# Involution stage of a two-layer vision kernel: the next block's logit chain starts four taps before the slot, evenly spread, and the sums are turned back between two chains

## The reference, cut to what matters

```python
n, _, h, w = x.shape
x1 = conv1x1(x, w1, b1)
x2 = conv1x1(x, w2, b2)
x3 = conv1x1(x, w3, b3)
p = conv1x1(position(h, w, x.dtype), wp, bp)
sub2 = x1[:, :, None] - unfold_patches(x2)
subp = p[:, :, None] - unfold_patches(p)
...
y = jax.nn.relu(bn_eval(feat, bn1_g, bn1_b, bn1_m, bn1_v))
y = conv1x1(y, cw1)
y = jax.nn.relu(bn_eval(y, bn2_g, bn2_b, bn2_m, bn2_v))
wgt = conv1x1(y, cw2, cb2)
wgt = jax.nn.softmax(wgt, axis=2)
...
        out = out + patch * wgt[:, :, idx][:, :, None]
```

## Time and profile before

| | |
|---|---|
| median of 3 runs | 4714.37 us (4712.43 to 4714.96) |
| the profiled execution | 4718.02 us, span 4716.2 us |
| involution stage within it | about 180 to 2107 us |
| busy over the whole span | PE 88%, DVE 74%, ACT 45%, POOL 23% |
| mean granted TensorE clock | 0.961 |

### The profile page before, as it was taken

The page is one execution under the profiler, slowest core; times in us unless marked ns, Lnnn a source line. Parts: engine busy times, 40 slices in busy tenths (PEclk is TensorE's granted clock), DMA queues, the critical chain, the costliest instruction groups (busy, mean ns, idle before and its releaser), DMA issues. The chain is left out here.

```text
span 4716.2 us, 68009 instructions
## 1 busy us (share of the span) xinstructions
PE 4158.9 (88%) x25234; PEld 2496.8 (53%) x25234; DVE 3511.6 (74%) x3316; ACT 2110.5 (45%) x3376; POOL 1085.4 (23%) x426
## 2 busy tenths in 40 slices
PE   5789989899998989976889898898889879999999
PEld 2267777777777777763343433334344234444544
DVE  6179989899898989987566756756676358787877
ACT  1455545455554545423645455363544523232321
POOL 1265555555655555530000000000000000000000
PEclk9889999999999999998999999999999989999999
DMA  5400101101101011012011001102111010000100
GB/s 202 129 29 33 37 30 37 37 16 37 37 34 36 29 37 37 11 45 62 1 49 56 22 21 59 45 1 57 47 22 22 28 47 32 24 31 29 34 20 24
DMA packets 88774, 186.97 MB, mean 40 GB/s; under 512 B 14622, under 2 KB 78158, under 8 KB 85378
## 3 DMA queue, kind: packets, MB, share of 16 engines
q1 hardware_dynamic: 86274, 177.51, 11.9%
q0 software_dynamic: 1744, 4.89, 0.3%
q10 hardware_dynamic: 432, 0.20, 0.0%
HBM read 103.60 MB, written 59.70 MB: 35 GB/s over the span
## 5 line engine op out<-in xcount | busy, mean ns | idle before, releaser
L684 DVE TENSOR_TENSOR prod<-ps,win 128x1792 f32<-128x1792 f32 x686 | 1340.2, 2012 | 128.8 <-ACT ps L579 96.5
L752 PE MATMUL ps<-ident,prod 128*128 128x128 f32 x9604 | 1185.5, 279 | 150.4 <-DVE prod L684 126.5
L752 PEld LDWEIGHTS ps<-ident,prod 128*128 128x128 f32 x9604 | 1104.5, 144 | 313.5 <-DVE prod L684 173.0
L1129 ACT ACTIVATE phq<-ps 128x896 f32<-128x896 f32 x448 | 384.2, 917 | 200.3 <-PE ps L1390 199.5
L594 ACT ACTIVATE y<-ps,u2c,s2c 128x392 f32<-128x392 f32 x392 | 265.4, 677 | 442.3 <-PE ps L735 440.9
L1225 DVE TENSOR_TENSOR phk<-kv 128x2048 f32<-128x2048 f32 (+1 forms) x200 | 455.9, 2283 | 0.6
L470 POOL TENSOR_TENSOR lg<-lg,mx 128x1568 f32<-128x1568 f32 x98 | 348.7, 3569 | 338.1 <-DVE mx L673 338.1
L465 POOL TENSOR_TENSOR y<-a1w,x2w 128x1568 f32<-128x1568 f32 x98 | 320.3, 3269 | 427.8 <-PE ps L735 408.9
L1551 POOL MEMSET ones<- 128x128 bf16 x1 | 0.2, 204 | 1654.0 <-POOLq L894 1654.0
L734 PE MATMUL ps<-y,cw1bd 128*128 128x392 f32 x784 | 331.4, 505 | 52.3 <-ACT y L587 29.5
L1762 PE MATMUL ps<-xn,w_s 128*128 128x448 f32 x896 | 353.5, 549 | 6.2 <-ACT hid L1599 6.2
(11 more groups left out here) (220 smaller groups left out, 5058.9 us busy)
## 6 DMA issues: line engine op xcount, KB each, us to landing
win<-planes SPq DMA_DIRECT2D x14, 2480.0 KB, 9.4
qst<-qsp SPq DMA_DIRECT2D x96, 196.0 KB, 4.6
planes<-stage SPq DMA_DIRECT2D x7, 1984.0 KB, 7.0
xs<-in_x SPq DMA_DIRECT2D x8, 1568.0 KB, 21.1
conv_dram<-osb SPq DMA_DIRECT2D x14, 896.0 KB, 4.9
t<-in_x SPq DMA_DIRECT2D x28, 448.0 KB, 4.1
xn<-conv_dram SPq DMA_DIRECT2D x28, 448.0 KB, 6.9
t_dram<-tout SPq DMA_DIRECT2D x28, 448.0 KB, 2.9
```

The source lines that it names most:

```text
L684: v.tensor_tensor(prod[b.buf(t)][:].rearrange("p (s h w) -> p s h w", h=RW, w=W), w, xw, ALU.mult).then_inc(prod_ready, 1)
L752: mm = pe.matmul(acc[:, at:at + P], x[:, at:at + P], ident[:], start=(t == 0 and k % 4 == 0), stop=(t == NU - 1), is_transpose=True, skip_ ...
L1129: act.activation(dst, src, ACT.Square).then_inc(phq_done, 1)
```

## The change

`slot` gets a third block, `n`, whose chain begins in the last four taps: `CH_AT` goes from -4 to 39 in steps of 8/5 tap, so that chunks 0, 1 and 2 of the next block stand at taps 45, 46 and 48, and the last logits at tap 41. The running maxima and the fold (tap 43) move with it. The sums are turned back at taps 41 to 44, between the two chains, copied at 42 to 45, and scaled at 47; the inverse stands at tap 1 of the next slot. The denominators are added up in `osb` instead of `acct`. On GpSimd shifts 1 and 2 stand directly at the slot's start, behind shift 0, the first two subtractions of `n` stand behind `total`, and the exponential of row 1 moves from the last tap to the first tap of the next slot. The loads of x2, a1 and two feature rows move to the end of the slot before. The slot list has three slots ahead of the loop, five turns of two slots, and three behind it. The copies at the slot's end (`weights`) stay where they were.

```diff
@@ -327,20 +327,19 @@
 SUMC = SHARE * PW
 NBACK = (SUMC + 511) // 512
 HALF = 1024
-GAP = 8
-CH_AT = [1 + c * 6 // 5 for c in range(GAP)] + [16 + c * 6 // 5 for c in range(NCH - GAP)]
+FIRST = -4
+CH_AT = [FIRST + c * 8 // 5 for c in range(NCH)]
 LAST_LOGIT = CH_AT[-1] + 2
-LOGIT_AT = CH_AT[1:] + [LAST_LOGIT]
-MAX_AT = [min(LOGIT_AT[CPI * i + CPI - 1] + 3, LAST_LOGIT + 1) for i in range(K7)]
+MAX_AT = [CH_AT[CPI * i + CPI] + 3 if i + 1 < K7 else LAST_LOGIT + 1 for i in range(K7)]
 FOLD_AT = MAX_AT[-1] + 1
-EXP_NOW = {FOLD_AT + 3: 0, NU - 1: 1}
-EXP_NEXT = {3: 2, 5: 3, 9: 4, 16: 5, 22: 6}
-SHIFT_BEFORE = {1: (1,), 2: (2, 3), 3: (4,), 4: (5,), 5: (6,)}
-BACK_AT = [CH_AT[GAP] - 5 + p for p in range(NBACK)]
-RECIP_AT, SCALE_AT = BACK_AT[-1] + 3, BACK_AT[-1] + 5
+EXP_NOW = FOLD_AT + 3
+EXP_NEXT = {0: 1, 5: 2, 10: 3, 17: 4, 23: 5, 30: 6}
+BACK_AT = [LAST_LOGIT + p for p in range(NBACK)]
+RECIP_AT, SCALE_AT = 1, BACK_AT[-1] + 3
+FIRST_RELU = NU + FIRST - 3
 PAIRS = (TAPS + 1) // 2
-ADD_BEFORE = {4: (1, 2), 5: (3,), 6: (4, 5)}
 NADD = K7 + 3
+assert BACK_AT[-1] < NU + FIRST
...
         half = run[:, 0:3]
-        wsum = acct[:, 0:K7 * PW].rearrange("p (j x) -> p j x", x=PW)
+        wsum = osb[:, 0:K7 * PW].rearrange("p (j x) -> p j x", x=PW)
...
-            slot(Blk(0, 0), None)
-            slot(Blk(0, 1), Blk(0, 0))
-            with eng.Fori(0, NW // 2 - 1) as it:
-                slot(Blk(it, 2), Blk(it, 1))
-                slot(Blk(it, 3), Blk(it, 2))
-            slot(None, Blk(0, NW - 1))
+            slot(None, None, Blk(0, 0))
+            slot(Blk(0, 0), None, Blk(0, 1))
+            slot(Blk(0, 1), Blk(0, 0), Blk(0, 2))
+            with eng.Fori(0, NW // 2 - 2) as it:
+                slot(Blk(it, 2), Blk(it, 1), Blk(it, 3))
+                slot(Blk(it, 3), Blk(it, 2), Blk(it, 4))
+            slot(Blk(0, NW - 2), Blk(0, NW - 3), Blk(0, NW - 1))
+            slot(Blk(0, NW - 1), Blk(0, NW - 2), None)
+            slot(None, Blk(0, NW - 1), None)
...
-                        pool.wait_ge(turned, NBACK * b.n)
+                        pool.wait_ge(stored, 16 * b.n)
...
-            def slot(a, b):
-                for i in range(K7):
-                    if b:
-                        for k in SHIFT_BEFORE.get(i, ()):
-                            shift(b, k)
-                        for k in ADD_BEFORE.get(i, ()):
-                            add(b, k)
-                    if a:
-                        z(a, i)
+            def slot(a, b, n):
                 if b:
-                    add(b, K7 - 1)
+                    shift(b, 1)
+                    shift(b, 2)
+                if a:
+                    z(a, 2)
+                if b:
+                    shift(b, 3)
+                if a:
+                    z(a, 3)
+                if b:
+                    shift(b, 4)
+                    add(b, 1)
+                if a:
+                    z(a, 4)
+                if b:
+                    shift(b, 5)
+                    add(b, 2)
+                    add(b, 3)
+                if a:
+                    z(a, 5)
+                if b:
+                    shift(b, 6)
+                    add(b, 4)
+                if a:
+                    z(a, 6)
+                if b:
+                    add(b, 5)
+                    add(b, 6)
                     total(b)
+                if n:
+                    z(n, 0)
+                    z(n, 1)
                 if a:
                     shift(a, 0)
...
+            def slot(a, b, n):
+                if a:
+                    load_win(a)
+                    for i in range(2, K7):
+                        features(a, i)
+                if n:
+                    load_x(n)
+                    features(n, 0)
+                    features(n, 1)
+                if b and not b.early(1):
+                    store(b.n - 1)
+                if b and not (a or n):
                     store(b.n)
...
-                if k == 0:
-                    act.wait_ge(wadd, NADD * (m + 1))
...
-            def give(m, p):
+            def give(m, p, total):
                 act.wait_ge(turned, NBACK * m + p + 1)
                 if p == 0:
                     act.wait_ge(stored, 16 * (m + 1))
+                    act.wait_ge(wadd, NADD * total)
...
+            def chunk(a, c):
+                second(a, c)
+                if c >= 1:
+                    third(a, c - 1)
+                if c % CPI == CPI - 2 and c // CPI + 1 < K7:
+                    first(a, c // CPI + 1)
+
...
-                    if a and u == 0:
-                        first(0)
+                    if n and u == FIRST_RELU:
+                        first(n, 0)
                     if a and u in CH_AT:
-                        c = CH_AT.index(u)
-                        second(c)
-                        if c >= 1:
-                            third(c - 1)
-                        if c % CPI == CPI - 2 and c // CPI + 1 < K7:
-                            first(c // CPI + 1)
+                        chunk(a, CH_AT.index(u))
+                    if n and u - NU in CH_AT:
+                        chunk(n, CH_AT.index(u - NU))
                     if a and u == LAST_LOGIT:
-                        third(NCH - 1)
-                    if a and u in EXP_NOW:
-                        expo(a, EXP_NOW[u])
+                        third(a, NCH - 1)
+                    if a and u == EXP_NOW:
+                        expo(a, 0)
...
-                    if b and not b.early(1):
-                        v.wait_ge(turned, NBACK * b.n)
...
-                if not a:
+                if b and not (a or n):
+                    v.wait_ge(divided, 2 * b.n)
...
                 pe.wait_ge(acc_out, 2 * m + 1 + p // 2)
                 if a and p == 0:
-                    pe.wait_ge(relu2, a.g(GAP))
+                    pe.wait_ge(relu2, a.g(NCH))
                 if a and p == 1:
-                    pe.wait_ge(logit, a.g(GAP - 1))
+                    pe.wait_ge(logit, a.g(NCH))
...
+                if c == 0 and not a.early(3):
+                    pe.wait_ge(back_out, NBACK * (a.n - 2) - 1)
...
+                if c == 0 and not a.early(3):
+                    pe.wait_ge(back_out, NBACK * (a.n - 2))
...
                     if a and u in CH_AT:
-                        c = CH_AT.index(u)
-                        first(c)
-                        if c >= 1:
-                            second(c - 1)
+                        chunk(a, CH_AT.index(u))
+                    if n and u - NU in CH_AT:
+                        chunk(n, CH_AT.index(u - NU))
                     if a and u == LAST_LOGIT:
-                        second(NCH - 1)
+                        second(a, NCH - 1)
```

109 lines of the change are left out of this document (51 added, 58 removed).

## The result

| | before | changed |
|---|---|---|
| median | 4714.66 us (8 runs, 4712.12 to 4725.05) | 4703.4 us (8 runs, 4698.83 to 4711.7) |
| ratio to before | | 0.9973, 95% interval 0.9963 to 0.9983 |
| span of the profiled execution | 4716.2 us | 4705.7 us |
| mean granted TensorE clock | 0.961 | 0.960 |

The changed kernel is faster by 0.27%, with 4703.4 us where 4702 was forecast.

The account below looks back on a forecast made before the run. TensorE and VectorE, both nearly full, were taken to bound the slot by waiting for each other. Start -8.5, slots +12, second slot -6.0, end +4.3 and returns -14 gave -12, so 4702 us, range 4658 to 4730.

Parts of the forecast that it names:

- The walk through the end of the chain: From TensorE's unit 41 on: fold at 4.6, unit 47 at 21.2, product 0 from 27.0, unit 1 ending at 34.0 us.
- The held scale: VectorE's scale at tap 47 starts inside GpSimd's third shift, waits 2.8 us and so takes 4.8 instead of about 2.
- The maxima: VectorE's running maxima wait for GpSimd: maxima 1, 2, 3 and 5 held 2.4, 0.9, 2.5 and 1.4 us, the fourth free.
- Tap 11's gap: Product 11 comes 1.0 us late for TensorE, the only stall expected between taps 2 and 40.
- rival 1: VectorE becomes the bound between taps 11 and 37; two us of extra waiting a slot give 4726 us; chance 0.17.
- The clock: Lower granted TensorE clock behind the gap before unit 47 adds 1.2 us a slot, between 0 and 2.3.
- the slots' term: Slots take 132.2 us, 1.0 more than the 131.2 before, the lower clock included.
- The returns: Four loop returns at 5 us replace five at 6.85, a term of -14 us; the skill's rule would give -7.
- Start and end: First product at 259.5, first fold 8.5 us earlier; the last 122 us grow by 4.3 for the scales.
- Rival 2: The scale isn't held, so the gap before unit 47 shrinks: -4.0 us in 11 slots, 4658 us; chance 0.12.
- rival 3: TensorE's clock stays up behind the gap before unit 47: -1.2 us in 11 slots, 4689 us; chance 0.14.
- rival 4: Even load absorbs all waits at the end of the chain: 124 us a slot, about 4610 us; chance 0.03.

Follow-up runs that it names:

- experiment 3: Changed kernel with ScalarE's first weights of the next slot put ahead of the early chunk at tap 48 and its relu: 4683.77 us.
- experiment 4: Changed kernel with the scale behind the slot's last product and the first weights ahead of the third early chunk: 4639.25 us.
- experiment 1: Changed kernel with GpSimd's shift 2 moved behind the subtraction of row 2: 4668.12 us.
- experiment 2: Changed kernel with VectorE's scale moved behind the slot's last product: 4682.09 us.
- experiment 9: Changed kernel with 20 repeated transposes on TensorE filling the gap ahead of unit 47: 4706.41 us.
- experiment 7: Changed kernel with scale last, weights first, and repeated transposes filling TensorE's gaps ahead of units 42 and 43: 4628.88 us.
- experiment 5: Changed kernel with the involution's slots written out straight instead of a loop: 4687.78 us.
- experiment 6: Kernel before the change, with its six loop turns written out straight: 4686.17 us.
- experiment 8: Changed kernel with scale last, weights first, repeated transposes ahead of units 42 and 43, and no loop: 4602.66 us.

## Why the prediction was right, and where it wasn't

- **The walk through the end of the chain: right.** From the fold (its start is 4.6 on the prediction's clock) unit 47 was put at 16.6 and stands at 16.63; product 0 at 22.4, measured 22.45; the end of unit 1 at 29.4, measured 29.4 (1062.22 + 1.53). The gap ahead of unit 47 was 3.17 for 3.4, product 0's wait 3.94 for 4, the slot without clock 130.86 for 131.0.
- **The held scale: right**, 4.83 for 4.8. The row it came from was a maximum that met an addition; it holds for a scale and a shift alike, two operations with two SBUF inputs each.
- **The maxima: nearly.** They took 4.17, 2.55, 4.08, 1.78 and 1.79 us: held for 2.4, 0.8, 2.4, 0 and 0, where 2.4, 0.9, 2.5, 0 and 1.4 were walked out. The fifth begins at 1145.78, just as GpSimd's subtraction ends (1142.53 + 3.26). Tap 11's gap is 0.75 for 1.0, and there is no other, so rival 1 never came near.
- **The clock: its size.** 1.2 us a slot was taken; it is 1.4 in 7 of 11 slots, 0.9 (in the table above the three without a return count in the slots' term, the four others in the returns'). The mechanism was right. What the prediction did not see is the other side: once the waits behind it go, the same slow stretch costs 2.0 to 2.8 us a slot (experiments 3 and 4). It had priced "the clock stays up" at 1.2 as if that were the most it could give.
- **The returns: wrong in size.** The count was right (4 for 5), but a return costs 6.92 by the table's count and some 5.8 without the clock at unit 47, where 5 was taken. Of "ScalarE's and TensorE's stalls are the old ones, but the wait for product 0 covers some; I take 5" the first part failed: TensorE waits 6.39 to 7.78 for "issue" where the kernel before has 2.46 to 4.21, and ScalarE 4.79 to 5.23 for 2.24 to 3.23. Why they grew isn't shown by any run. The second part fits the runs: with units 43 to 47 at the full clock a return costs 4.8 to 6.7 us where product 0 waits (experiments 1, 2 and 9), and 7.3 to 9.2 where it doesn't (4 and 7). The longer wait of product 0 in the returned slot shown above (5.63 against 3.94) is no sign of the return: it is 5.3 to 5.6 behind a slow unit 47 without one, too. The Trainium skill ("Runtime: NRT & Kernel Launch", Instruction fetch mechanics) states that a taken branch out of the loaded blocks stalls and that kernels are better unrolled where they can be. By its rule the term would be -7; measured it is -6.9 by the table's count, and by experiments 5, 6 and 8 unrolling is worth 26 to 40 us at the stage's end. The prediction had that sentence and rated it below its own guess.
- **The two misses cancel.** Slots -8.3 against the forecast, returns +7.1. Had only one been wrong, the time would have been 4694 or 4709. That the sum came out within 1.4 us of the median was luck.
- **Start and end.** Fold 1 -8.7 for -8.5: the first product stands at 260.24 for 259.5, after a load of the exponential's table (1.28 us, at 254.45; at 246.60 in the kernel before) that now stands right ahead of that exponential. The end cost 2.4 for 4.3; the last blocks' scales meet no shift and take 2.01.
- **The rivals.** Rival 2's 4658 became a program at 4668 (experiment 1), rival 3, the clock that stays up, one with 9.4 us less at fold 13, where it was priced at 13, and none less in the median (experiment 9), and rival 4's 124 us a slot one at 124.3 (experiments 7 and 8): the even load does what it promised, once nothing holds it up.

## What to carry to other kernels

An even spread of the load pays only if the in-order queues around it let it: here it could free 7 us of a slot of 131, and two instructions in the wrong place (a third shift ahead of a subtraction, a weights copy behind an early chunk) took all of it; the clock behind the gaps that are left takes up to 2 more (experiment 4). When work is moved, list for each engine what now stands ahead of the instruction that another engine waits for, and for VectorE and GpSimd also what is in progress at the same time. A slow stretch of TensorE's clock costs nothing while TensorE then waits for something that doesn't stand behind it (unit 42), and much once that wait is gone (unit 43 in experiment 4) or where what others wait for stands behind it (the early chunk behind unit 47). So after removing waits look at the granted clock again, and try filling the gaps that remain with work that is thrown away: it gave 10 us of 4639 in experiment 7, and nothing in the median in experiment 9.
